# Every second copy of the first feed-forward product moved from ScalarE to VectorE, in blocks of six and eight key tiles

## What is computed

```python
# attention: 16 heads of two 16-wide score maps each, 8 key/value heads
q, k, v = h @ Wq.T, h @ Wk.T, h @ Wv.T              # h = layernorm(x); rope on q and k
scores = q @ k.T * Dh ** -0.5 + causal              # (b, 32, 1024, 1024)
probs = softmax(scores)
diff = probs[:, :, 0] - lambda_full * probs[:, :, 1]
attn = rms_norm(diff @ v) * subln_weight * (1 - LAMBDA_INIT)
x = x + attn @ Wo.T
# feed forward: ternary weights, 512 -> 2048 -> 512
w1_q, w2_q = absmean_quant(w1), absmean_quant(w2)   # sign(w) * (|w| >= 0.7 * mean|w|)
h = gelu(layernorm(x) @ w1_q.T + b1)
out = x + h @ w2_q.T + b2
```

## Time and profile before

| | before |
|---|---|
| median of three runs | 4198.97 us |
| the profiled execution: time | 4199.09 us |
| its span, first to last instruction | 4197.2 us |
| PE busy | 3491.2 us (83%) |
| DVE busy | 3189.3 us (76%) |
| ACT busy | 2885.2 us (69%) |
| POOL busy | 1776.2 us (42%) |

### The profile page before, as it was taken

One profiled execution on the slowest core, in us unless ns is written; L12 is line 12 of the kernel. 1 busy time (PEld: TensorE's weight loads), 2 busy tenths in 40 slices (PEclk: granted clock), 3 DMA queues, 4 the chain that ended last, 5 costly groups with the idle time before them and its releaser, 6 DMA issues.

```text
span 4197.2 us, 84069 instructions
## 1 busy us (share of the span) xinstructions
PE 3491.2 (83%) x23454; PEld 2099.4 (50%) x23454; DVE 3189.3 (76%) x5170; ACT 2885.2 (69%) x6784; POOL 1776.2 (42%) x2333
## 2 busy tenths in 40 slices
PE   2688888888888888888888888888888888888886
PEld 1355554555444555455545555555545555555553
DVE  6777877778678886788767887778867778677882
ACT  1577766777667775677766777667766777667772
POOL 1244443454334543345432544334443444334543
PEclk6899999999999999999999999999999999999999
DMA  3101011000011001000011010111001010110000
GB/s 133 38 19 34 20 34 34 29 20 26 29 34 34 18 28 38 29 25 29 21 34 34 20 34 16 36 31 34 20 30 34 22 31 20 35 34 29 20 28 14
DMA packets 146840, 128.57 MB, mean 31 GB/s; under 512 B 66608, under 2 KB 117680, under 8 KB 145840
## 3 DMA queue, kind: packets, MB, share of 16 engines
q1 hardware_dynamic: 146352, 122.79, 9.1%
HBM read 67.61 MB, written 55.12 MB: 29 GB/s over the span
## 4 chain that ended last, share of the span: by engine, by line
PE 42%; DVE 22%; issue 19%; ACT 12%; POOL 2%; ACTq 1%; DVEq 1%; DMA 1%; SPq 0%; POOLq 0%
PE M L864 9%; PE F L936 7%; DVE NM L707 7%; PE SP_ L879 6%; PE M L914 5%; PE F L953 5%; PE DP L891 4%; DVE NM L715 4%; DVE E L734 3%; ACT E L579 3%; ACT DT L591 2%; PE M L858 2%; ACT L579 2%; ACT L596 1%; PE DX L891 1%
## 5 line engine op out<-in xcount | busy, mean ns | idle before, releaser
L579 ACT ACTIVATE E<-SP_,NM 128x256 f32<-128x256 f32 (+7 forms) x2048 | 1523.5, 744 | 922.6 <-DVE NM L715 527.2
L707 DVE TENSOR_REDUCE NM<-SP_ 128x1 f32<-128x896 f32 (+3 forms) x1024 | 1031.7, 1018 | 291.9 <-PE SP_ L880 286.5
L879 PE MATMUL SP_<-KST,QST 96*128 96x512 f16 (+3 forms) x3072 | 828.2, 341 | 372.1 <-ACT E L579 316.0
L734 DVE SCALAR_TENSOR_TENSOR E<-E,CC 128x512 f32<-128x512 f32 (+7 forms) x1024 | 941.4, 919 | 49.3 <-POOL CC L494 30.0
L891 PE MATMUL DP<-ident,E 128*128 128x128 f32 x3328 | 569.6, 286 | 85.7 <-DVE E L734 76.2
L879 PEld LDWEIGHTS SP_<-KST,QST 96*128 96x128 f16 x3072 | 274.4, 101 | 712.4 <-ACT E L579 487.1
L591 ACT ACTIVATE DT<-DP 128x512 f32<-128x512 f32 (+3 forms) x1024 | 525.7, 513 | 123.2 <-PE DP L891 117.0
L491 POOL TENSOR_TENSOR RP<-SUM,minus 128x1 f32<-128x1 f32 x512 | 292.5, 571 | 722.5 <-ACT E L579 708.2
L715 DVE TENSOR_REDUCE NM<-SP_ 128x2 f32<-128x1024 f32 (+3 forms) x512 | 419.2, 819 | 198.9 <-PE SP_ L880 188.9
L864 PE MATMUL M<-WQKV,WT 128*128 128x512 f32 x1040 | 546.0, 618 | 17.9 <-DVE TOK L775 11.0
L936 PE MATMUL F<-X2H,W1Q 128*128 128x256 f16 x2048 | 499.6, 282 | 31.3 <-DVE SQ L803 16.6
(11 more groups left out here) (96 smaller groups left out, 4847.3 us busy)
## 6 DMA issues: line engine op xcount, KB each, us to landing
scratch<-SPL SPq DMA_DIRECT2D x65, 576.0 KB, 2.8
QST<-scratch SPq DMA_DIRECT2D x390, 64.0 KB, 2.4
X<-in_x SPq DMA_DIRECT2D x66, 256.0 KB, 2.8
out<-SQ SPq DMA_DIRECT2D x64, 256.0 KB, 2.0
KST<-scratch SPq DMA_DIRECT2D x390, 32.0 KB, 1.9
DT<-in_w2T SPq DMA_DIRECT2D x1, 4096.0 KB, 25.9
KST<-in_w1T SPq DMA_DIRECT2D x2, 1024.0 KB, 10.6
WQKV<-in_wqT SPq DMA_DIRECT2D x1, 1024.0 KB, 6.6
```

Of the source, the lines that this page charges most:

```text
L579: act.activation(dst, score_out(i, 2 * n + k, w), ACT.Exp, bias=NM[:, (2 * u + k) % 8:(2 * u + k) % 8 + 1], scale=1.0, accum_out=SUM[:, i ...
L707: nc.vector.tensor_reduce(NM[:, m:m + 1], score_out(i, 2 * n + k, P * (i + 1)), AX.X, ALU.max, negate=True).then_inc(max_ready, 1)
L734: nc.vector.scalar_tensor_tensor(out=E1[:, u % 4, 0:w], in0=E2[:, u % 2, 0:w], scalar=CC[:, u % 4:u % 4 + 1], in1=E1[:, u % 4, 0:w], op0=A ...
L879: pe.matmul(SP_[:, k[a // 512], 0:n], q, KST[0:ROWS, a // P:(a + n) // P, kk, :], start=True, stop=not last)
```

## The change

In blocks with t >= 5, which for the first product means t = 5 and t = 7, pieces k = 1, 3, 5 and 7 are copied by DVE and not by ACT. These fall on half steps 6, 13, 22 and 29. DVE does them with `tensor_scalar` (times 1 / XS, plus the bias column) at the end of its half step: behind the row maximum, behind `diff` where there is one, and behind `rest` at half step 22. It waits for the product (`f1_ready`) and for POOL's split of four pieces before (`h_ready`) as ACT did, and counts the same `hp_ready`. In each of eight sequences this is two blocks of four pieces, 64 pieces or 128 instructions in all. Nothing else is moved.

```diff
+    def by_vector(self, k):
+
+        return self.t >= 5 and k % 2 == 1
...
# act_work
                     piece = T.first_product(hs)
-                    if piece and piece[1] == 2:
+                    if piece and piece[1] == 2 and not T.by_vector(piece[0]):
                         k, n = piece[0], 8 * T.pair + piece[0]
                         after(act, f1_ready, n + 1)
                         after(act, h_ready, n - 3)
...
# dve_work, behind LN2_REST and ahead of OUT_AT
+                    piece = T.first_product(hs)
+                    if piece and piece[1] == 2 and T.by_vector(piece[0]):
+                        k, n = piece[0], 8 * T.pair + piece[0]
+                        after(dve, f1_ready, n + 1)
+                        after(dve, h_ready, n - 3)
+                        for f in (2 * k, 2 * k + 1):
+                            ins = nc.vector.tensor_scalar(HP[:, f % GELU_F, :], F[:, 2 * P * (f % 2):2 * P * (f % 2) + 2 * P],
+                                                          1.0 / XS, b1c[:, f:f + 1], ALU.mult, ALU.add)
+                        ins.then_inc(hp_ready, 1)
```

## The result

The changed kernel takes 4216.75 us (median of five runs, 4214.46 to 4218.62) against 4198.97 us before (4194.09 to 4203.26): a ratio of 1.0044, interval 1.0029 to 1.0058. That is slower by 17.8 us. The sign is as forecast and the time is inside the range, but the forecast was +10. The profiled execution took 4214.46 us with a span of 4212.7 us, 15.4 us above the one shown of before.

A forecast was written before the change was run, and what follows sets the result against it. The loop of scores, row maximum and exponential bounds the kernel where PE runs out of work. Per sequence +0.91 us (t = 5) and +0.29 (t = 7), eight times plus tail 10.2 us, gave 4209 us, range 4197 to 4220.

The forecast's parts named there:

- The price c: Time by which a pair of copies holds DVE up: 0.79 us, with bounds 0.66 and 0.96.
- Pieces 1 and 3: Half steps 6, 13: gain 0.36 (t = 5) or 0.45 us (t = 7), then cost 0.79; net +0.43, +0.34.
- The zero cover of maximum 14: Half step 14: row maximum and exponential come 0.79 us later, PE is held likewise, and nothing hides it.
- The list of waits: PE waits at half steps 7, 17, 25 and the block's end; otherwise no gaps over 60 ns.
- (d): Half step 7: PE's small wait of 0.17 us for ACT's copy of piece 1, which would go.
- Piece 5 at t = 5: Half step 22: ACT was last, so exponential 23 starts earlier and PE's wait at half step 25 shrinks: -0.15 us.
- Piece 5 at t = 7: Half step 22: exponential 0.05 us earlier; DVE's next difference and maximum 24 are 0.79 us late, meeting no PE wait.
- Piece 7 at t = 5: Half step 29: row maximum 30 and exponential 30 come later, passed on to the next block: +0.63 us.
- Piece 7 at t = 7: Half step 29: delay hidden under PE's 3.84 us wait for the next keys; 0.6 us once in the last sequence.
- The sum: +0.91 us at t = 5, +0.29 at t = 7; over eight sequences 9.6, with the tail 10.2 us.
- The clock: Rival: longer PE waits behind Gelu and at block end keep clock low: +9 us, 4218; chance 0.15, shared with dearer copies.
- Faster: Rival: the loop hangs on ACT, not DVE, so ACT's freed 0.71 us pays: 19 us faster, 4180; chance 0.10.

The follow-up runs named there:

- e1: The change cut to piece 1 on DVE, the other three left on ACT: 4180.27 us, 0.9957 of the kernel before.
- moved code: Kernel before with 6 or 24 do-nothing semaphore increments in DVE's code of sequence 0: 4188.19 us (0.9978) or 4184.96 us (0.9976).
- e6: The change with all four pieces' copies put behind the next row maximum (piece 7 behind the difference of half step 31): 4182.86 us, 0.9962 of before.
- e4: The change cut to piece 7 on DVE, the other three left on ACT: 4200.13 us, 1.0001 of the kernel before.

## Why the forecast was right, and where not

**The price c.** Forecast 0.79, measured 0.79 (copies' start to maximum's start), 475 ns a copy as put together. The lower value of 0.62 for c is out.

**Pieces 1 and 3.** Right in size and place: -0.34 and +0.78 at t = 5 by the waits' ends; maximum 14 of t = 7 comes +0.34 later on the mean of six blocks (32.83 to 33.17 us from the block's start), as forecast. The zero cover of maximum 14 held, the wait behind the Gelu kept its length (3.79 us at t = 7; 3.59 before and 3.68 after at t = 5), and PE's new waits for exponential 14 are 0.51 us (t = 5) and 0.73 (t = 7) against 0.8 and 1.0 expected. Exponential 14 starts at 2547.16, 0.03 us behind the maximum's 1.21 us, as it did in the earlier trace rows.

**The list of waits.** "PE is otherwise without gaps over 60 ns there" isn't so. Two us behind the start of each block PE waits 2.76 us (t = 5) or 3.12 (t = 7) for an exponential, and 0.31 us for ACT's `WT` ahead of (d). Both are the same before and after, so the sum doesn't suffer by it.

**Piece 5 at t = 5.** Forecast -0.15, measured 0.0 in the change and -0.08 alone. The wait at half step 25 went from 1.15 to 1.06 us, as said. The rest is below what can be read with the stalls moved.

**Piece 5 at t = 7.** The step by which DVE's next work (difference, maximum 24) "is c late and meets no PE wait" failed: +0.47 against -0.05. The difference was not c late but 1.25 us, as it ran into POOL's split. The prediction followed PE's, DVE's and ACT's rows there; POOL's stood in the same window and were not followed. 8 x 0.5 = 4 us.

**Piece 7 at t = 5.** +0.63 measured in the change, exactly the forecast (from the last score wait to the end 4.61 us before, 5.24 after).

**Piece 7 at t = 7.** The step "the same delay is hidden: PE waits 3.84 us for keys" failed: +0.77 against 0. The prediction itself priced this: "if that cover were gone, it would cost 8 x 0.6 = 5 us". It is 8 x 0.77 = 6 us. The cover was read off PE, which waits for two things at the block's start, and the other one, DVE's chain over X2H and X2L, had no slack. The earlier trace rows showed this chain at t = 5. The rows of DVE at t = 7 of sequence 4 were read before the forecast and show it too, but with a gap that the profile puts down to PE:

```profile
2586.79 0.69 DVE L796 SCALAR_TENSOR_TENSOR X2L<-M,X2H 128x512 f16<-128x512 f32 x1 [1.13 <-ACT X2H L630]
2590.12 0.42 DVE L715 TENSOR_REDUCE NM<-SP_ 128x2 f32<-128x256 f32 x1 [2.64 <-PE SP_ L880]
```

PE's scores there start at 2587.94 and the maximum 2.18 us later, where in sequence 0 it is 0.51 us (564.32 to 564.83). So DVE did not stand for the scores; the keys could have come somewhat later at no cost, and X2L could not.

**The sum.** With the two failed steps put right the forecast's own sum is 9.6 + 4 + 6 = 20 us; at equal clock t = 5 and t = 7 measure 17 against before, in which lie the stalls that went away, and 8 x (1.12 + 1.55) = 21 against moved code.

**The place of the code.** Not in the prediction at all: -7 to -10 us. "I am wrong ... if blocks without copies change" was its test, and t = 2 did change, by -0.74 us. This error had the other sign and hid most of the first two, so the forecast's nearness to the result (10 against 17.8) owes something to luck.

**The clock.** Given as a rival with +9 us; it came true beside the forecast, not in place of it: 5 to 10 us. "The t = 5 block shown is at 0.95 with a wait of nearly the same length" spoke against it, and that block does stay at 0.95 in both; the five others of the loop's six did not (10.2 us low, 72.0 to 72.3 us long).

**Faster.** "ACT, not DVE, is what the loop hangs on" is false for pieces 3 and 7 as placed, and true for piece 1 (e1). With the copies behind the maximum, ACT's freed time is worth something (e6), which the rival didn't foresee.

## What to carry to other kernels

A step is covered only if the engine that it delays has slack, so for each delayed engine follow its own chain to the next common point; another engine's long wait for a transfer is no cover for it. The price of a moved operation is what stands behind it: against moved code, the same 475 ns copies make a t = 5 block 1.1 us longer ahead of the row maxima and 0.7 us shorter behind them. Before a difference of 0.2% is put down to an edit, run the old kernel with its code shifted by a few idle instructions, since here that alone was worth as much.

## What the runs showed of the hardware

DVE stands 0.3 to 0.5 us at fixed instructions of a loop, with no wait in the profile that explains it, and six idle instructions ahead of the loop move these stalls to other instructions (7 us of 4195; with 24 it is 9). ACT has such stalls too (0.20 us in e4). A DVE operation on two SBUF operands and a POOL operation on SBUF lengthen each other, by how their starts lie: 1.27 to 2.25 us for the one, 1.15 to 2.00 for the other. At a turn of the loop DVE stands 2.4 to 4.1 us between its last instruction and its first, where it stands 0.0 to 0.1 in code that is written out. And 24 idle matmuls in a wait of PE, 2.8 us of work, make the kernel 13 to 23 us faster: the stretches at the lower clock behind that wait are gone.
